# A graph network on one core: GpSimd's wait in the edge loop moved to the middle of a step and put on VectorE's turn of the step in front

## The chip, the cores and the metric

One NeuronCore of a Trainium2 chip. The metric is the time of one execution on the device, in microseconds (us); lower is better. The profiled execution and the timed runs are different executions of the same program.

## What is computed

Four layers of message passing on a graph with 6250 nodes and 206,250 directed edges, 64 channels, all in float32. The edges are sorted by target. In one layer:

```
msg   = relu(h[src] + e) + 1e-7            # one row of 64 per edge; e = edge_attr @ w + b
m     = msg * t
ex    = exp(m - segment_max(m, dst)[dst])
alpha = ex / segment_sum(ex, dst)[dst]
agg   = segment_sum(msg * alpha, dst)
out   = relu(layernorm((h + agg) @ w1 + b1)) @ w2 + b2
```

A small encoder stands before the layers, and layers 1 to 3 take `relu(layernorm(h))` and add their result to `h`. The gather `h[src]` fetches a 256-byte row of a table in HBM for every edge, once in each layer.

## The kernel before

**Streams and steps.** The edges are cut into four streams of equal length, each of which lies on 32 partitions (lanes). A *step* (`chunk` in the code) takes 256 edges of each stream. A layer has 202 steps, numbered k = 0 to 201; over all layers the number is n = 202 * layer + k. Two neighbouring steps make a pair, for which the large transfers are made. Layer 0 is written out apart from layers 1 to 3, which share one loop body: there `layer` is a register, and in layer 0 it is the Python number 0. The first four steps of a layer and the last ones are written out too, with k known, and those between are in a loop of four steps.

**A step, engine by engine.**
- GpSimd gathers the table's rows: eight indirect DMAs (L543), b = 0 to 7, each of 128 rows and 32 KB, into one of four places, that of n mod 4 (`gathered`, two buffers of two halves). Each adds 16 to the semaphore `rows_in[i]`, i = n mod 4. The last step of a layer has only four such blocks (`LAST_BLOCKS` = 4).
- VectorE waits for `rows_in` and *turns* the step (`turn_edges`, L1140, a stream transpose from `gathered` into PSUM), which adds 1 to `turn_done`. After that the place in `gathered` may be written again. It adds the edge terms (L1149), takes the running maxima (scans, L1161), the differences (L1175), the weighting (L1180), the running sums (scans, L1188 and L1193), and turns the sums into `rows_out` (L1203).
- ScalarE does the ReLUs and exponentials, and copies the indices of a later pair (`copy_idx`, `idx_ready`).
- SyncE has, for each pair, a store of `rows_out` (1024 KB), a load of `edges` (640 KB) and a store of `track` (513 KB). The first waits for `rows_ready`, which VectorE's L1203 gives, the other two for `scanned`, which its maxima (L1161) give.

**VectorE's order.** In the loop VectorE works on several steps at a time (`chunk` in its block): maxima of n-2, the turn of n, the turned sums of n-4, differences of n-2, weighting of n-3, edge terms of n, sums of n-3. From step 196 on (`CLOSE` = 197) the order is another: for k = 198 to 201 it is

```python
for k in range(CLOSE + 1, CHUNKS):
    peak(k - 1)      # maxima and differences
    leave(k - 2)     # turned sums, L1203
    turn(k)          # L1140
    add(k)
    sums(k - 1)      # weighting and sums
```

**GpSimd's order.** Its instructions are in order. `hold` is a wait for a semaphore followed by an increment of `pool_passed`, which nobody waits for in the loop. Ahead of the first step of a pair it holds for the indices; ahead of every step from k = 2 on it holds for `turn_done` to reach n - 1, which says that step n - 2 has been turned. The place that step n writes was last read by the turn of step n - 4.

At the end of a layer GpSimd waits for the stores of `track`, gathers a few rows for the streams' seams (L554, `head_parts`), and then one row for every node (L572).

Of the kernel before, what the change touches and what calls it, by code (L numbers as in the profile page):

```python
# [19 lines left out]
BLOCKS = N // LANES  # L20
# [62 lines left out]
def build_program(nc, x, src, dst, dst_blocks, few, ids, attr, enc_w, edge_w, w1, w2, rows, columns, final_row, consts, out):  # L83
# [17 lines left out]
    with ctx:  # L101
# [3 lines left out]
        def sem(name):  # L105
            return ctx.enter_context(nc.semaphore(name))
# [152 lines left out]
        turn_done = sem("turn_done")  # L259
# [64 lines left out]
        pool_passed = sem("pool_passed")  # L324
# [11 lines left out]
        def hold(eng, passed, s, count):  # L336

            if not (isinstance(count, int) and count <= 0):
                eng.wait_ge(s, count)
                eng.sem_inc(passed, 1)  # L340

        def chunk_quads(eng, layer, body, tail=2):

            for i in range(4):
                body(layer * CHUNKS + i, i, 0, i, False)
            with eng.Fori(1, (CHUNKS - tail) // 4) as j:
                for i in range(4):
                    body(layer * CHUNKS + 4 * j + i, 4 * j + i, j, i, False)
            for k in range(CHUNKS - tail, CHUNKS):
                body(layer * CHUNKS + k, k, k // 4, k % 4, k == CHUNKS - 1)  # L350
# [24 lines left out]
        def table_stores(layer):  # L375

            return 16 * (GROUPS + NODE_GROUPS * layer)

        def all_layers(eng, body):
            body(0)  # L380
            with eng.Fori(1, LAYERS) as layer:
                body(layer)
# [4 lines left out]
        def counts_until(t):  # L387

            g = t // GROUP
            done = sum(len(group_of(i)) for i in range(g % 2, g, 2)) + t - GROUP * g + 1
            return (counted_dve if g % 2 else counted_act), done
# [125 lines left out]
        @block.gpsimd  # L519
        def _(pool):  # L520
            for t in range(SEEK):
                hold(pool, pool_passed, block_found, t // GROUP + 1)
                if t >= GROUP:
                    hold(pool, pool_passed, *counts_until(t - GROUP))
                pool.indirect_dma_start(
                    found_rows[t % GROUP], None, dst_blocks,
                    bass.IndirectOffsetOnAxis(ap=block_i[:, t:t + 1], axis=0)).then_inc(block_in[t % GROUP], 16)

            def layer_body(layer):
                hold(pool, pool_passed, table_out, table_stores(layer))  # L530

                def chunk(n, k, j, i, last):
                    u, st = i // 2, i % 2
                    if st == 0:
                        hold(pool, pool_passed, idx_ready, PAIRS * layer + (2 if isinstance(k, int) and k == 0 else 2 * j + u + 1))

                    if not isinstance(k, int) or k >= 2:

                        hold(pool, pool_passed, turn_done, n - 1)
                    for b in range(LAST_BLOCKS if last else BLOCKS):  # L540
                        at = W * st + C * b
                        col = BLOCKS * st + b
                        pool.indirect_dma_start(  # L543
                            gathered[u][:, at:at + C], None, table,
                            bass.IndirectOffsetOnAxis(ap=idx_s[u][:, col:col + 1], axis=0)).then_inc(rows_in[i], 16)

                chunk_quads(pool, layer, chunk)

                for u in range(2):
                    hold(pool, pool_passed, track_stored[u], 16 * SLOT_PAIRS[u] * (layer + 1))  # L550
                if isinstance(layer, int):
                    pool.wait_ge(head_ready, 1)
                for i in range(4):
                    pool.indirect_dma_start(  # L554
                        head_parts[:, i:i + 1], None, tracks,
                        bass.IndirectOffsetOnAxis(ap=head_i[0:HEADS, i:i + 1], axis=0)).then_inc(heads_in, 16)
                for u in range(2):
                    hold(pool, pool_passed, rows_stored[u], 16 * SLOT_PAIRS[u] * (layer + 1))
                for i in range(2):
                    pool.indirect_dma_start(  # L560
                        head_rows[:, C2 * i:C2 * i + C2], None, state[0:EDGE_ROWS, :],
                        bass.IndirectOffsetOnAxis(ap=head_row_i[0:TARGETS, i:i + 1], axis=0)).then_inc(heads_in, 16)
                hold(pool, pool_passed, empty_out, 16)
                if isinstance(layer, int):
                    pool.wait_ge(end_ready, 1)
                hold(pool, pool_passed, merged_stored, 16 * (layer + 1))
                for i in range(NODE_GROUPS):

                    if i >= 2:
                        hold(pool, pool_passed, pre_ready, layer * NODE_GROUPS + i - 1)  # L570
                    for tile in range(FIRST[i], FIRST[i] + WIDTHS[i]):
                        pool.indirect_dma_start(  # L572
                            ends[:, tile, :], None, state,
                            bass.IndirectOffsetOnAxis(ap=end_i[:, tile:tile + 1], axis=0)).then_inc(ends_part[i], 16)

            all_layers(pool, layer_body)
# [903 lines left out]
```

## Time and profile before

| | |
|---|---|
| median of 3 runs | 8689.54 us (8688.6 to 8689.72) |
| the profiled execution | 8691.99 us |
| its span | 8690.2 us |
| VectorE busy | 6377.8 us (73%) |
| GpSimd busy | 6358.8 us (73%) |
| ScalarE busy | 3267.7 us (38%) |
| TensorE matmuls busy | 1037.5 us (12%) |

The span is that of the profile; the execution's own time is 1.8 us longer. In the profile's rows PE is TensorE, DVE is VectorE, ACT is ScalarE, POOL is GpSimd and SP is SyncE; the Lxxx is the line of the kernel. A gather's row on POOL is the time in which GpSimd makes the transfer's descriptors; the data land later.

### The profile page before, as it was taken

To read this page: it belongs to the slowest core of one execution; us is meant where nothing else is said; L and a number is where in the kernel's file an instruction comes from. 1 tells how busy PE (TensorE), PEld (TensorE's weight loads), DVE (VectorE), ACT (ScalarE), POOL (GpSimd) and SP (SyncE) were. 2 spreads that over 40 slices of the span, in tenths; PEclk is the share of its full clock that TensorE was granted. 3 is DMA by queue.
4 is the path that set the end of the run, shared out by engine and by line. 5 is a ranking of instruction groups with operands and counts; after the bars stand their busy time and mean duration, and the time that the engine had idled before them with its cause. 6 is when DMAs were issued, how large, how long until landed. Compare 5 with 4: busy or idle time off the path is not lost.

```text
span 8690.2 us, 45214 instructions
## 1 busy us (share of the span) xinstructions
PE 1037.5 (12%) x3019; PEld 763.4 (9%) x3019; DVE 6377.8 (73%) x10058; ACT 3267.7 (38%) x7146; POOL 6358.8 (73%) x6723
## 2 busy tenths in 40 slices
PE   4333333332200000000110000000020000000002
PEld 3222222221200000000110000000020000000002
DVE  6777777777677777777767777777776777777776
ACT  4444444443433333333333333333343333333334
POOL 6777777776677777777667777777756777777775
PEclk6655555555555555555555555555555555555555
DMA  6566555564244444444334444444433444444443
GB/s 202 206 206 206 203 201 203 202 203 163 89 136 136 138 139 139 139 139 136 120 97 139 138 135 136 138 139 139 139 109 105 139 139 138 135 136 137 139 139 106
DMA packets 444022, 1287.55 MB, mean 148 GB/s; under 512 B 164252, under 2 KB 178245, under 8 KB 366149
## 3 DMA queue, kind: packets, MB, share of 16 engines
q1 hardware_dynamic: 226516, 1049.15, 34.4%
q0 software_dynamic: 217456, 237.95, 10.8%
q14 instruction: 43, 0.34, 0.0%
q8 instruction: 7, 0.11, 0.0%
HBM read 574.47 MB, written 712.10 MB: 148 GB/s over the span
## 4 chain that ended last, share of the span: by engine, by line
POOL 24%; issue 16%; DVE 13%; DMA 13%; ACT 8%; PE 2%; POOLq 0%; ACTq 0%; DVEq 0%
POOL gathered L543 23%; DMA gathered<-node_table,idx_s 12%; DVE rows_out L1203 4%; ACT track L785 3%; DVE psum L1180 2%; DVE psum L1149 2%; ACT psum L792 2%; DVE psum L1175 2%; ACT psum L808 1%; DVE psum L1140 1%; PE psum L673 1%; PE psum L665 0%; ACT idx_s L776 0%; ACT square_junk L855 0%; POOL arena L572 0%
## 5 line engine op out<-in xcount | busy, mean ns | idle before, releaser
L543 POOL DMA_INDIRECT gathered<-node_table,idx_s x6448 | 6091.2, 945 | 2066.7 <-issue 1902.7
L800 ACT ACTIVATE decay<-psum 128x512 f32<-128x512 f32 (+1 forms) x808 | 481.7, 596 | 4893.2 <-DVE psum L1175 4893.2
L1140 DVE STREAM_TRANSPOSE psum<-gathered 128x512 f32<-128x512 f32 (+1 forms) x808 | 582.5, 721 | 2063.9 <-DMA gathered<-node_table,idx_s 2063.5
L1161 DVE TENSOR_TENSOR_SCAN track<-psum,track,edges 128x256 f32<-128x256 f32 (+1 forms) x1616 | 1107.3, 726 | 0.0
L1188 DVE TENSOR_TENSOR_SCAN run<-decay,run,psum 128x256 f32<-128x256 f32 (+1 forms) x1616 | 1100.4, 720 | 0.0
L1193 DVE TENSOR_TENSOR_SCAN run<-decay,run,psum 128x256 f32<-128x256 f32 (+1 forms) x1616 | 1094.5, 718 | 0.0
L1203 DVE STREAM_TRANSPOSE rows_out<-run 128x1024 f32<-128x1024 f32 (+1 forms) x808 | 970.3, 1201 | 0.1
L588 PE MATMUL psum<-attr_s,edgew_s 128*128 128x256 f32 x1616 | 748.4, 643 | 1259.8 <-ACT made_s L710 1246.2
L785 ACT ACTIVATE track<-psum,bias_col 128x256 f32<-128x256 f32 (+1 forms) x1616 | 678.7, 471 | 223.2 <-DVE psum L1149 174.8
L651 PE MATMUL psum<-cst,tails 128*3 128x128 f32 x48 | 10.9, 415 | 6160.6 <-DVE tails L1284 6091.0
L588 PEld LDWEIGHTS psum<-attr_s,edgew_s 128*128 128x128 f32 x1616 | 503.1, 326 | 1503.4 <-ACT made_s L710 1375.1
L1149 DVE TENSOR_TENSOR psum<-psum,edges 128x512 f32<-128x512 f32 (+1 forms) x808 | 558.4, 691 | 1.0
L1180 DVE TENSOR_TENSOR psum<-track,psum 128x512 f32<-128x512 f32 (+1 forms) x808 | 552.9, 684 | 3.3 <-ACT psum L808 3.2
L792 ACT ACTIVATE psum<-track,t_col 128x512 f32<-128x512 f32 (+1 forms) x808 | 551.5, 682 | 0.9
L651 PEld LDWEIGHTS psum<-cst,tails 128*3 128x3 f32 x48 | 5.6, 121 | 6165.8 <-issue 6162.4
L1175 DVE TENSOR_TENSOR psum<-track,psum 128x512 f32<-128x512 f32 (+1 forms) x808 | 538.3, 666 | 1.0
L807 ACT ACTIVATE decay<-decay 128x512 f32<-128x512 f32 (+1 forms) x808 | 506.2, 626 | 0.9
L808 ACT ACTIVATE psum<-psum 128x512 f32<-128x512 f32 (+1 forms) x808 | 480.1, 594 | 0.0
L801 ACT ACTIVATE psum<-psum 128x512 f32<-128x512 f32 (+1 forms) x808 | 477.5, 591 | 0.0
L572 POOL DMA_INDIRECT arena<-edge_state,end_i x196 | 185.2, 945 | 112.5 <-issue 65.8
L1337 DVE RECIPROCAL psum<-arena 128x448 f32<-128x448 f32 (+2 forms) x32 | 83.5, 2611 | 75.9 <-DMA arena<-edge_state,end_i 75.2
L710 ACT ACTIVATE made_s<-psum 128x512 f32<-128x512 f32 x202 | 119.1, 590 | 8.6 <-PE psum L588 8.6
(177 smaller groups left out, 1370.9 us busy)
## 6 DMA issues: line engine op xcount, KB each, us to landing
edge_state<-rows_out SPq DMA_DIRECT2D x404, 1024.0 KB, 5.1
edges<-edge_rows SPq DMA_DIRECT2D x406, 640.0 KB, 6.8
tracks<-track SPq DMA_DIRECT2D x404, 513.0 KB, 8.0
gathered<-node_table,idx_s POOLq DMA_INDIRECT x6448, 2.4
edge_rows<-made_s SPq DMA_DIRECT2D x101, 640.0 KB, 6.8
attr_s<-in_attr SPq DMA_DIRECT2D x101, 512.0 KB, 7.7
made_s<-resets SPq DMA_DIRECT2D x101, 128.0 KB
node_table<-tab SPq DMA_DIRECT2D x27, 224.0 KB, 2.5
```

Of the source, the lines that this page charges most:

```text
L543: pool.indirect_dma_start(gathered[u][:, at:at + C], None, table, bass.IndirectOffsetOnAxis(ap=idx_s[u][:, col:col + 1], axis=0)).then_inc ...
L588: last = pe.matmul(made_ps[:, N * q:N * q + N], edgew_s[:, col:col + P], attr_s[u][:, at:at + N], start=(half == 0), stop=(half == 1))
L785: last = act.activation(message[u][:, at:at + width], turned[s][:, N * q:N * q + width], ACT.Relu, bias=bias_col[:, q:q + 1])
L792: act.activation(halves(logit[s])[:, :, 0:width], halves(message[u])[:, :, N * st:N * st + width], ACT.Copy, scale=t_col[:, :]).then_inc(l ...
L1140: v.transpose(turned[s].rearrange("p (q b e) -> p b q e", q=2, e=LANES)[:, 0:blocks], gathered[u][:, W * st:W * st + C * blocks]).then_inc ...
L1149: v.tensor_tensor(sums, sums, halves(edges[u][:, W * st:W * st + W])[:, :, 0:width], ALU.add).then_inc(summed, 1)
L1161: last = v.tensor_tensor_scan(maxima[u][:, at:at + width], logit[s][:, N * q:N * q + width], reset_s[u][:, N * st:N * st + width], carried ...
L1175: v.tensor_tensor(logits, before, logits, ALU.subtract).then_inc(diff_done, 1)
L1180: v.tensor_tensor(halves(wmsg)[:, :, 0:width], halves(message[u])[:, :, N * st:N * st + width], halves(weight[s])[:, :, 0:width], ALU.mult ...
L1188: v.tensor_tensor_scan(run[s][:, N * q:N * q + width], decay[s][:, N * q:N * q + width], weight[s][:, N * q:N * q + width], run[1 - s][:, ...
L1193: last = v.tensor_tensor_scan(run[s][:, W + N * q:W + N * q + width], decay[s][:, N * q:N * q + width], wmsg[:, N * q:N * q + width], run[ ...
L1203: v.transpose(rows_out[u][:, 2 * W * st:2 * W * st + 2 * W].rearrange("p (b x c) -> p x b c", x=4, c=LANES)[:, :, 0:blocks], run[s][:, :]. ...
```

## The change

In layer 0 nothing changes. In layers 1 to 3 the hold for `turn_done` ahead of a step goes away. In its place one stands between the fourth and the fifth gather (b = 4) of every step but k = 0, and it is for `turn_done` to reach n, which says that step n - 1 has been turned.

```diff
-                    if not isinstance(k, int) or k >= 2:
+                    first = isinstance(layer, int)
+                    if first and (not isinstance(k, int) or k >= 2):
 
                         hold(pool, pool_passed, turn_done, n - 1)
                     for b in range(LAST_BLOCKS if last else BLOCKS):
+                        if not first and b == BLOCKS // 2 and not (isinstance(k, int) and k == 0):
+
+                            hold(pool, pool_passed, turn_done, n)
                         at = W * st + C * b
                         col = BLOCKS * st + b
                         pool.indirect_dma_start(
```

`first` is true in layer 0. `BLOCKS // 2` is 4. The last step's loop runs over b = 0 to 3 only.

## Rows read from the trace of the kernel before

**Rows 1.** The page, costliest groups: busy us, mean ns | idle before them.

```profile
L543 POOL DMA_INDIRECT gathered<-node_table,idx_s x6448 | 6091.2, 945 | 2066.7 <-issue 1902.7
```

**Rows 2.** Windows, layer 1's loop: busy us (instructions) of PE, PEld, DVE, ACT, POOL.

```profile
2270.00:4210.00 1940.00, 0.00 (x0) 0.00 (x0) 1447.70 (x2224) 699.52 (x1456) 1466.86 (x1554) 0.50 0.42 137
```

**Rows 3.** Waits of VectorE, same window: us in total, times, longest.

```profile
DVE psum L1140 <- DMA gathered<-node_table,idx_s: 495.5, 193, 7.3
```

**Rows 4.** Timeline, a pair of steps in layer 1's loop: start us, us.

```profile
4001.75 0.35 SPq L465 DMA_DIRECT2D edge_state<-rows_out  x1
...
4007.34 0.94 POOL L543 DMA_INDIRECT gathered<-node_table,idx_s  x1 [0.30 <-issue]
...
4011.34 0.73 DVE L1140 STREAM_TRANSPOSE psum<-gathered 128x512 f32<-128x512 f32 x1 [4.10 <-DMA gathered<-node_table,idx_s]
...
4013.59 0.94 POOL L543 DMA_INDIRECT gathered<-node_table,idx_s  x1 [0.30 <-issue]
...
4019.77 0.73 DVE L1140 STREAM_TRANSPOSE psum<-gathered 128x512 f32<-128x512 f32 x1 [0.97 <-DMA gathered<-node_table,idx_s]
```

**Rows 5.** Timeline, the end of layer 1's edge loop.

```profile
4227.06 0.69 DVE L1140 STREAM_TRANSPOSE psum<-gathered 128x512 f32<-128x512 f32 x1
...
4238.82 0.68 DVE L1140 STREAM_TRANSPOSE psum<-gathered 128x512 f32<-128x512 f32 x1
...
4240.31 0.95 POOL L543 DMA_INDIRECT gathered<-node_table,idx_s  x1 [2.07 <-DVE psum L1140]
...
4246.55 0.69 DVE L1140 STREAM_TRANSPOSE psum<-gathered 128x512 f32<-128x512 f32 x1
...
4252.44 0.34 SPq L424 DMA_DIRECT2D edges<-edge_rows  x1
...
4254.04 0.95 POOL L543 DMA_INDIRECT gathered<-node_table,idx_s  x1 [0.30 <-issue]
...
4254.21 0.68 DVE L1140 STREAM_TRANSPOSE psum<-gathered 128x512 f32<-128x512 f32 x1
...
4261.94 0.42 DVE L1140 STREAM_TRANSPOSE psum<-gathered 128x256 f32<-128x256 f32 x1
```

**Rows 6.** Windows, within the end of layer 1's edge loop.

```profile
4226.00:4260.00 34.00, 0.00 (x0) 0.00 (x0) 33.80 (x51) 15.28 (x31) 20.78 (x22) 0.50 0.58 189
```

**Rows 7.** Timeline, start of layer 1: turn of step 0, b4 of step 1.

```profile
2251.09 0.73 DVE L1140 STREAM_TRANSPOSE psum<-gathered 128x512 f32<-128x512 f32 x1 [8.76 <-DMA gathered<-node_table,idx_s]
...
2254.96 0.94 POOL L543 DMA_INDIRECT gathered<-node_table,idx_s  x1 [0.30 <-issue]
```

**Rows 8.** Timeline, a pair of steps in layer 3's loop.

```profile
7170.12 0.73 DVE L1140 STREAM_TRANSPOSE psum<-gathered 128x512 f32<-128x512 f32 x1 [5.20 <-DMA gathered<-node_table,idx_s]
...
7171.17 0.94 POOL L543 DMA_INDIRECT gathered<-node_table,idx_s  x1 [0.30 <-DVE psum L1140]
```

**Rows 9.** The chain: ahead of layer 1's first gather, and of its head_parts.

```profile
2238.91 1.08 issue
...
4267.27 4.17 DMA tracks<-track
4271.65 0.75 issue
```

**Rows 10.** L543 alone, whole execution: landings of its transfers.

```profile
DMA to landing us min/median/max: 2.3/2.4/8.1
```

**Rows 11.** L543 alone, last gather of layers 1, 2, 3: start, landing.

```profile
DMA to landing us min/median/max: 4.9/4.9/4.9
...
L543 POOL DMA_INDIRECT gathered<-node_table,idx_s x1: 946/946/946, 6401.6 to 6401.6; - x1
...
DMA to landing us min/median/max: 5.1/5.1/5.1
...
L543 POOL DMA_INDIRECT gathered<-node_table,idx_s x1: 943/943/943, 8550.5 to 8550.5; - x1
...
DMA to landing us min/median/max: 5.2/5.2/5.2
```

**Rows 12.** Timeline of VectorE, end of layers 2 and 3: turn of step 200.

```profile
6401.77 0.68 DVE L1140 STREAM_TRANSPOSE psum<-gathered 128x512 f32<-128x512 f32 x1
...
8550.60 0.69 DVE L1140 STREAM_TRANSPOSE psum<-gathered 128x512 f32<-128x512 f32 x1
```

## The prediction

> **What bounds the kernel now.** I read the page first [rows 1]: GpSimd's gathers (L543) are 6448 instructions of 945 ns, with 2066.7 us of short pauses between them, and nearly all of those pauses are not put down to a wait. The windows view of one layer's loop gives GpSimd's rate [rows 2]: 1940 us for 1554 gathers, 1.248 us each, so 9.99 us for a step of 8. In the same stretch VectorE waits 495.5 us, about 5 in each pair of steps, all of it ahead of its turn of a step (L1140) and for a gather [rows 3]. So GpSimd feeds VectorE.
>
> The timeline of a pair shows where they lie [rows 4]. I call a step by its number in its layer (0 to 201), b0 to b7 its gathers. The numbering is read backwards from the end of the layer: the last four gathers are step 201's, the pause before the row at 4240.31 stands at step 200's b0 [rows 5], and from there it goes by 1.249 us. So 4007.34 is b7 of step 176 and 4008.59 would be b0 of 177. The turn of 176 starts at 4011.34, 4.0 us after b7, because SyncE's three large transfers, the first issued at 4001.75, delay the landing; the turn of 177 starts at 4019.77, 2.43 us after b7 of 177 (4007.34 + 8 x 1.249 = 4017.34). Even steps are turned late and odd ones early, but GpSimd never pauses: its 0.30 us between gathers is there whether or not it had a wait to pass. Its queue is filled far ahead of it, so today's wait (turn of n-2 before b0 of n) is passed long before the gather is due: the turn of 176 ends at 4012.07, and step 178 begins four gathers after the row at 4013.59, at 4018.59, 6.5 us later.
>
> At the end of a layer VectorE leaves this rhythm. Steps 197 to 201 are done in another order, and the window 4226 to 4260 has 33.80 us of VectorE work in 34.00 us [rows 6]. There VectorE sets the end, not GpSimd.
>
> **The change, part by part.** No work is added. In layers 1 to 3 each step from 1 to 200 waits once, as steps 2 to 201 did before, now ahead of b4 and for the turn of n-1. Step 201 has four gathers, never comes to b4, and has no wait.
>
> *What a passed wait costs.* Where GpSimd did pause, the turn of 198 ran 4238.82 + 0.68 = 4239.50, and the gather held by it started at 4240.31 [rows 5]: 0.81 us from the end of the turn to the gather, after an empty queue. From there to the gather at 4254.04 it is 13.73 us for 11 gathers, 1.248 each, so running dry doesn't slow the ones behind it.
>
> *In the loop, odd n* (held by a late, even turn). Turn of 176 ends 4012.07, plus 0.81 is 4012.88; b4 of 177 now starts at 4013.59 [rows 4]. It is in time by 0.71 us. *Even n*: 4019.77 + 0.73 + 0.81 = 4021.31 against b4 of 178 at 4013.59 + 8 x 1.25 = 4023.59, 2.28 us in time. So the typical pair loses nothing, but on the odd side the margin is thin. I subtracted the same way for all 591 pairs of an L1140 and an L543 row in the three loops (steps 1 to 197 of each; the first pair of layer 1 stands in [rows 7]: 2251.09 + 0.73 + 0.81 = 2252.63 against 2254.96): odd margins have a mean of 0.64 us and go below zero some ten times, the worst being the turn at 7170.12 [rows 8]: 7170.85 + 0.81 = 7171.66 against 7171.17, 0.49 us late. The shortfalls sum to 0.1, 0.2 and 0.7 us: **1.0 us** for the three layers. A shortfall moves GpSimd, the next turn and the next large transfers alike, so the margin afterwards is the same: they add, and don't feed themselves. The other bound is a slower restart: ahead of a layer's first gather the chain has 1.08 us where the quick one has 0.75 [rows 9]. With all margins 0.33 us smaller the same sum is about 11 us. I take the quick one, since it is the in-loop case.
>
> *At the end of the layer* (layer 1; all from rows 5). The turns of 197, 198, 199, 200 start at 4227.06, 4238.82, 4246.55, 4254.21 and last 0.69. Step by step:
> - b4 of 198 would be due at 4223.5, and now waits for the turn of 197: 4227.75 + 0.81 = 4228.56. b7 at 4232.3. Landed long before 4238.82.
> - b0 of 199 follows at 4233.55, b3 at 4237.3. b4 waits for the turn of 198: 4240.31, the very time at which step 200 begins today. b7 at 4244.06; a quiet landing (2.4 us [rows 10]) is 4246.5, and VectorE wants it at 4246.55. No or little loss. Should it land up to 2.9 us later, that delay lies inside the next one, and adds at most 0.6 us.
> - b0 of 200 at 4245.31, b3 at 4249.05. The turn of 199 is over at 4247.24, so b4 to b7 go on without pause: b7 at 4254.05. That is four gathers later than today (4240.31 + 7 x 1.249 = 4249.05), and it is the time of today's last gather of all, which stands at 4254.04. It starts behind SyncE's transfers of 4252.44 and just after, triggered by scans of VectorE that lie ahead of the turn of 200 and don't move. So I take that gather's landing: 4.9 us [rows 11], 4259.0. VectorE wants it at 4254.21. **Late by 4.8 us.**
> - Step 201's four gathers end at 4259.05, land by 4261.5 to 4264, and are wanted at 4261.94 + 4.8. No further loss.
>
> Everything behind the turn of 200 on VectorE is in order and has no idle time to give back, and GpSimd's next instruction (the head_parts gather) comes behind a 4.17 us transfer of tracks that VectorE's last scan triggers [rows 9]. So the 4.8 us reach the end of the layer. Layers 2 and 3 have the same shape [rows 11, 12]: today's last gather at 6401.6 lands after 5.1 us = 6406.7 against a turn at 6401.77 (4.9); 8550.5 + 5.2 = 8555.7 against 8550.60 (5.1). Together 14.8 us, and 0.03 us of reaction each: **14.9 us**.
>
> The landing is the one disputed price. Its bounds are 2.4 us (the median of all) and 5.2 us. With 2.4 the gather lands at 4256.45, 2.2 us late, and three layers cost 6.6. I take 5, because those very rows start at the same point behind the same transfers.
>
> The Trainium skill (DMA: Bandwidth & Descriptors, section on the anatomy of one DMA on the gpsimd path) gives such a transfer about 2.0 us plus its bytes over 436 GB/s. For 32 KB that is 2.08 us by the page, an estimate; the quiet 2.4 us of this trace is near it, the 4.9 to 5.2 us behind large transfers are not. By the page each layer would lose 1.9 us and the whole change come to about 6.8 us.
>
> **Sum.** 1.0 + 14.9 = 15.9 us. The profiled execution took 8691.99 (span 8690.2 and 1.8 around it), and becomes 8707.9. It stands 2.5 above the median of the runs, so the median goes from 8689.54 to **8705.4**, 0.18% more. Nothing can be gained in the loop: GpSimd makes no pause there that a later wait could remove.
>
> **Rivals.**
> - *The loop stalls too.* If a wait in the middle restarts as slowly as a layer's first gather, or large transfers jitter more once GpSimd has no lead, the odd margins of 0.64 us are used up. At 0.33 us less it is 11 + 14.9 = 26 us, 8715.5; at 0.8 us less my pairs give 72 us, 8777. For it: the longest wait for a gather is 7.3 us in [rows 3], so late turns vary by microseconds. Against: every restart within the loop's end took 0.81.
> - *The last gather lands quietly.* Condition: the transfers of 4252.4 don't hold it. 1.0 + 6.6 = 7.6 us, 8697. Against: [rows 11].
> - *Nothing happens.* The 4.8 us would have to be hidden in the layer's end, or step 200's gathers be sent earlier than I count. 8689.5 to 8691. Against: the 33.80 busy of 34.00 [rows 6].
> - *Faster.* With fewer gathers queued the 1.249 us interval might shrink. It pays from 3.3 ns each (15.9 us over 4848 gathers); at 10 ns it is 8657. Against: the gathers after the restart, with nothing queued behind them, are 1.248 us apart.
>
> **How the numbers follow.** My forecast 0.66, its own range 8702.5 to 8710 (landings of 4.5 to 5.5 us, loop stalls of 0 to 5). Stalls in the loop 0.17, quiet landing 0.07, nothing 0.06, faster 0.04. A time can be told from no change here from about 0.2% on, 17.4 us, or 8706.9. My forecast lies just inside it: of its 0.66 I put 0.46 below and 0.20 above. Same: 0.46 + 0.07 + 0.06 = 0.59. Slower: 0.20 + 0.17 = 0.37. Faster 0.04. The range reaches down to the quiet landing (8696) and up to the slow restart (8716); outside are nothing, faster, and the worse half of the loop stalls, 0.18.
>
> **What would show it.** In the changed profile: GpSimd's interval stays 1.25 us in the three loops, with pauses over 0.35 us in some ten steps and none beyond 0.6; at a layer's end three pauses (b4 of 198, 5 us; b4 of 199, 2 to 3 us; then none until the layer's last gather, near 5 us later than today counted from the layer's start); VectorE idle for 4.8 to 5.1 us before the turn of 200, where it now has no idle time; the loop's waits of VectorE near 495 us. Layer 0 stays as it is. I am wrong if most pairs show a pause before b4, if that turn doesn't wait, or if the wait is given back before the layer ends.

## The result, and the profile of the changed kernel

Median 8706.93 us over 13 runs, against 8688.6 us over 13 runs of the kernel before: 18.3 us more, a ratio of 1.0022 with a 95% interval of [1.0014, 1.0029]. The forecast was 15.9 us more. The change makes the kernel slower, by 0.21%, just above the 0.2% from which the prediction takes a time as told from no change.

The profiled execution took 8706.93 us (span 8705.1), 14.9 us more than the one before (8691.99), which had been 3.4 us above the median of the 13 runs. On the page, the gathers have the same duration as in [rows 1] and their pauses add up to 22 us more; VectorE waits for them as before.

```profile
L547 POOL DMA_INDIRECT gathered<-node_table,idx_s x6448 | 6085.9, 944 | 2089.0 <-issue 2006.5
L1144 DVE STREAM_TRANSPOSE psum<-gathered 128x512 f32<-128x512 f32 (+1 forms) x808 | 582.6, 721 | 2081.5 <-DMA gathered<-node_table,idx_s 2081.5
```

(The change added four lines, so L543 is now L547 and L1140 is L1144.) The window over layer 1's loop, the same as in [rows 2], has the same 1554 gathers in 1940 us. The next line is the wait of VectorE there, 492.8 us against 495.5 in [rows 3]. In the loop, then, next to nothing has changed.

```profile
2270.00:4210.00 1940.00, 0.00 (x0) 0.00 (x0) 1447.16 (x2225) 699.49 (x1456) 1465.42 (x1554) 0.50 0.45 137
```

```profile
DVE psum L1144 <- DMA gathered<-node_table,idx_s: 492.8, 194, 8.0
```

Now the end of layer 1's edge loop, which answers to [rows 5]. All times here are about 2 us earlier than in the trace before, because the layer began that much earlier. Start us, us, engine, line, and in brackets the idle time before.

```profile
4225.05 0.68 DVE L1144 STREAM_TRANSPOSE psum<-gathered 128x512 f32<-128x512 f32 x1
4226.54 0.94 POOL L547 DMA_INDIRECT gathered<-node_table,idx_s  x1 [5.92 <-DVE psum L1144]
...
4236.82 0.68 DVE L1144 STREAM_TRANSPOSE psum<-gathered 128x512 f32<-128x512 f32 x1
4238.31 0.94 POOL L547 DMA_INDIRECT gathered<-node_table,idx_s  x1 [2.08 <-DVE psum L1144]
...
4244.57 0.73 DVE L1144 STREAM_TRANSPOSE psum<-gathered 128x512 f32<-128x512 f32 x1
...
4250.49 0.34 SPq L424 DMA_DIRECT2D edges<-edge_rows  x1
...
4252.03 0.94 POOL L547 DMA_INDIRECT gathered<-node_table,idx_s  x1 [0.30 <-issue]
...
4257.02 0.94 POOL L547 DMA_INDIRECT gathered<-node_table,idx_s  x1 [0.30 <-issue]
4257.26 0.73 DVE L1144 STREAM_TRANSPOSE psum<-gathered 128x512 f32<-128x512 f32 x1 [4.92 <-DMA gathered<-node_table,idx_s]
```

The four VectorE rows are the turns of steps 197, 198, 199 and 200 (4225.05, 4236.82, 4244.57, 4257.26; the first pause of GpSimd is ahead of b4 of 198, the second ahead of b4 of 199). In [rows 5] the turn of 200 came 7.66 us after that of 199 with no idle time; here it comes 12.69 us after, 4.92 of them idle. The last gather of step 200 (4252.03; the one at 4257.02 is the last of 201) goes 1.5 us after SyncE's load of edges. The chain of the three layers has what that gather took from its start to its landing:

```profile
4252.03 5.20 DMA gathered<-node_table,idx_s
...
6405.94 4.83 DMA gathered<-node_table,idx_s
...
8561.64 5.13 DMA gathered<-node_table,idx_s
```

In the window 4224 to 4258 VectorE now has 28.90 us of work, where [rows 6] had 33.80 in 34.00.

```profile
4224.00:4258.00 34.00, 0.00 (x0) 0.00 (x0) 28.90 (x42) 13.75 (x28) 22.64 (x24) 0.50 0.61 188
```

In the loops GpSimd makes some short pauses that weren't there. The worst is in layer 3, ahead of b4 of an odd step, and answers to [rows 8]: the turn that it waits for ends at 7339.86, and 0.80 us later the gather starts, in place of 0.30 us after its predecessor.

```profile
7339.00 0.94 POOL L547 DMA_INDIRECT gathered<-node_table,idx_s  x1 [0.30 <-issue]
7339.13 0.73 DVE L1144 STREAM_TRANSPOSE psum<-gathered 128x512 f32<-128x512 f32 x1 [5.09 <-DMA gathered<-node_table,idx_s]
7340.66 0.94 POOL L547 DMA_INDIRECT gathered<-node_table,idx_s  x1 [0.71 <-issue]
```

Counted over all rows of the gathers and turns, layer by layer (loop: steps 1 to 196, pauses above 0.35 us and what they have above 0.30; end: from the end of the turn of 196 to that of 200):

| layer | before: pauses, end | changed: pauses, end |
|---|---|---|
| 0 | 1 (0.4 us), 42.94 | 1 (0.4 us), 42.94 |
| 1 | 0, 42.88 | 7 (1.1 us), 47.98 |
| 2 | 0, 42.87 | 5 (1.0 us), 47.61 |
| 3 | 0, 42.88 | 10 (2.4 us), 47.91 |

The ends of layers 1 to 3 take 5.10, 4.74 and 5.03 us more, 14.9 together, and the loops' pauses come to 4.6 us. Their sum, 19.5, stands beside the 18.3 of the medians. The two profiled executions are only 14.9 us apart because the loops of layers 1 to 3 were themselves a little long in the trace before: from the turn of step 4 to that of 196 they took 1919.96 to 1920.49 us there, and 1918.5 to 1919.8 us in the other kernels whose loops have no pause. The changed kernel's took 1920.35, 1920.65 and 1921.87.

### The profile page after: what moved, and what is told of

Read it like the earlier page. It is cut to its first block, busy times and chain, and to the rows that moved or that the text cites. A ratio compares the mean times of both kernels' runs of the same rounds, so it can differ in the third digit from the quotient of the medians.

```text
span 8705.1 us, 45361 instructions
## 1 busy us (share of the span) xinstructions
PE 1039.3 (12%) x3019; PEld 770.2 (9%) x3019; DVE 6378.0 (73%) x10058; ACT 3267.4 (38%) x7146; POOL 6353.2 (73%) x6723
## 4 chain that ended last, share of the span: by engine, by line
POOL 44%; issue 21%; DMA 5%; DVE 3%; PE 2%; ACT 1%; POOLq 0%; DVEq 0%
POOL gathered L547 43%; DMA gathered<-node_table,idx_s 4%; DVE psum L1144 1%; PE psum L677 1%; PE psum L669 0%; ACT square_junk L859 0%; POOL arena L576 0%; PE psum L686 0%; DVE run L1197 0%; POOLq L346 0%; DVE run L1192 0%; DVE track L1165 0%; POOL head_parts L558 0%; DVE pre L1351 0%; DVE psum L1348 0%
## 5 line engine op out<-in xcount | busy, mean ns | idle before, releaser
L547 POOL DMA_INDIRECT gathered<-node_table,idx_s x6448 | 6085.9, 944 | 2089.0 <-issue 2006.5
L1144 DVE STREAM_TRANSPOSE psum<-gathered 128x512 f32<-128x512 f32 (+1 forms) x808 | 582.6, 721 | 2081.5 <-DMA gathered<-node_table,idx_s 2081.5
```

The costliest lines, as they stand in the source:

```text
L547: pool.indirect_dma_start(gathered[u][:, at:at + C], None, table, bass.IndirectOffsetOnAxis(ap=idx_s[u][:, col:col + 1], axis=0)).then_inc ...
L1144: v.transpose(turned[s].rearrange("p (q b e) -> p b q e", q=2, e=LANES)[:, 0:blocks], gathered[u][:, W * st:W * st + C * blocks]).then_inc ...
```

## Experiments

Each has runs of the kernel before beside it, from the same chip; "end" is the stretch of the table above, of layers 1, 2 and 3. Single runs of one kernel spread over some 8 us, so the ends and pauses in the traces say more than the medians here.

**Only the loop changed.** Steps 198 to 201 keep the wait of before; for that, the last six steps are written out.

```diff
-                    first = isinstance(layer, int)
-                    if first and (not isinstance(k, int) or k >= 2):
+                    moved = not isinstance(layer, int) and not (isinstance(k, int) and k >= 198)
+                    if not moved and (not isinstance(k, int) or k >= 2):
...
-                        if not first and b == BLOCKS // 2 and ...
+                        if moved and b == BLOCKS // 2 and ...
...
-                chunk_quads(pool, layer, chunk)
+                chunk_quads(pool, layer, chunk, tail=6)
```

> In layers 1 to 3 steps 1 to 197 wait as in the changed kernel (ahead of b4, for the turn of n-1), steps 198 to 201 as in the kernel before. My theory (the loop costs only the few short pauses of a margin that runs out, the end of a layer the rest): the three loops take 1 to 5 us longer together, the stretch from the turn of step 196 to that of 200 stays at 42.9 us, and the time is 1 to 5 us above the kernel before. Rival (every wait in the middle of a step costs a little): most of the 18 us stays.

8689.31 against 8687.22, ratio 1.0002 [0.9993, 1.0011]. Ends 42.89, 42.89, 42.88. Pauses 7, 4 and 3, together 2.9 us. The end is cured, and the short pauses of the loop stay. By the medians alone, 2.1 us can't be told from nothing.

**Only the end changed.** The same with `isinstance(k, int) and k >= 198` as the condition for `moved`.

> The reverse: only steps 198 to 200 have the changed wait (201 none), all others that of the kernel before. My theory: the loops are as before, from the turn of 196 to that of 200 it is 47.6 to 48.0 us in place of 42.9, three times, so 14 to 16 us above the kernel before. Rival (loop): within 3 us of the kernel before.

8701.85 against 8687.22: 14.6 us, ratio 1.0015 [1.0006, 1.0024]. Ends 47.71, 47.74, 47.90, 14.7 us above 42.88 together. No pause in the loops. With the run before this splits the change into its two parts: 14.6 and 2.1 by the medians.

**Only the place changed, not the turn that is waited for.**

```diff
-                        if not first and b == BLOCKS // 2 and not (isinstance(k, int) and k == 0):
+                        if not first and b == BLOCKS // 2 and not (isinstance(k, int) and k < 2):
 
-                            hold(pool, pool_passed, turn_done, n)
+                            hold(pool, pool_passed, turn_done, n - 1)
```

> The wait stands ahead of b4 in layers 1 to 3, but is still for the turn of step n-2. My theory: it is passed more than 10 us ahead of its gather in the loop, and at a layer's end the first pause comes later than before, so no difference: within 2 us of the kernel before, no pause of GpSimd in the loops. Rival (the place costs, since a wait breaks a run of gathers): 10 us or more above.

8687.52 against 8687.22, ratio 1.0 [0.9991, 1.0009]; ends 42.88, 42.88, 42.87; no pause in the loops. A wait within a step costs nothing by itself that these runs could show.

**The wait one gather earlier, ahead of b3.**

```diff
-                        if not first and b == BLOCKS // 2 and ...
+                        if not first and b == 3 and ...
```

> As the changed kernel, with the wait one gather earlier (ahead of b3). My theory: the mean margin of 0.64 us on the odd side becomes a lack of 0.6, so every odd step pauses; the pair is then even turn after odd turn 11.7 us, plus 0.81 restart, four intervals of 1.249, 2.43 landing and 0.73 turn, 20.65 in place of 19.98 us: 0.66 us x 98 pairs x 3 = 195 us, and about 18 us at the ends: 8900 us, give or take 25. Rival (the margin is no such quantity, a wait costs by its count): the time stays near 8707.

8915.89 against 8687.22: 228.7 us, ratio 1.0257 [1.0241, 1.0272]. One gather (1.25 us) of margin less makes the loss twelve times as large. The timeline in layer 1's loop:

```profile
3302.47 0.73 DVE L1144 STREAM_TRANSPOSE psum<-gathered 128x512 f32<-128x512 f32 x1 [4.12 <-DMA gathered<-node_table,idx_s]
3304.01 0.94 POOL L547 DMA_INDIRECT gathered<-node_table,idx_s  x1 [0.92 <-DVE psum L1144]
...
3311.38 0.73 DVE L1144 STREAM_TRANSPOSE psum<-gathered 128x512 f32<-128x512 f32 x1 [1.45 <-DMA gathered<-node_table,idx_s]
...
3323.46 0.73 DVE L1144 STREAM_TRANSPOSE psum<-gathered 128x512 f32<-128x512 f32 x1 [4.56 <-DMA gathered<-node_table,idx_s]
3324.99 0.94 POOL L547 DMA_INDIRECT gathered<-node_table,idx_s  x1 [1.32 <-DVE psum L1144]
...
3332.49 0.73 DVE L1144 STREAM_TRANSPOSE psum<-gathered 128x512 f32<-128x512 f32 x1 [1.57 <-DMA gathered<-node_table,idx_s]
```

Nearly every late (even) turn is followed by a pause of GpSimd, 3302.47 + 0.73 + 0.81 = 3304.01, and the odd turns wait longer than in [rows 4]. Over the loops an odd turn follows 9.00 us after the even one (sum of the forecast: 8.97) and an even one 11.63 to 11.72 after the odd one. There are 94 or 95 pauses in each layer. The loops take 63, 71 and 71 us more (forecast 65 each): where the even turns are at 11.72 a pair loses 0.72 us and not 0.66. The ends are 49.10, 48.90 and 49.16, 18.5 us more together (forecast 18). That is 223 us in the profile, 229 by the medians, against 213 and a bound of 238.

**Only step 199 changed**, in each of layers 1 to 3, with the last six steps written out as above.

```diff
+                    moved = not isinstance(layer, int) and isinstance(k, int) and k == 199
```

> In each of layers 1 to 3 one step alone, 199, has the changed wait, all others that of the kernel before. My theory: its b4 then goes at the time at which b0 of step 200 went, which puts step 200 four gathers later and its last gather behind SyncE's transfers, by itself: the whole 14 to 16 us, 4.7 to 5.1 in each layer. Rival (each of the changed waits at the end adds its share): about a third of it, 5 us.

8699.76 against 8686.73: 13.0 us, ratio 1.0015 [1.0006, 1.0024]. Ends 47.88, 47.71 and 48.09, as with all steps changed; no pause in the loops. Three waits of some 600 do the damage. In the timeline of layer 1's end GpSimd now stops once, ahead of b4 of 199, until the same time as with the changed kernel (end of the turn of 198 plus 0.81):

```profile
4236.42 0.68 DVE L1144 STREAM_TRANSPOSE psum<-gathered 128x512 f32<-128x512 f32 x1
...
4237.91 0.94 POOL L547 DMA_INDIRECT gathered<-node_table,idx_s  x1 [7.02 <-DVE psum L1144]
```

**The wait two gathers later, ahead of b6** (`b == 6`).

> As the changed kernel, with the wait ahead of b6. My theory: the odd margins of the loop grow by 2.5 us to about 3.1, so no pause there; at a layer's end step 200's last gather goes 2.5 us after its time before, at 4251.55 by the times of the kernel before, in front of SyncE's transfers of 4252.4, and lands about when the turn of 200 is due: 0 to 0.5 us late. In all 0 to 2 us above the kernel before. Rival (a late wait costs by its count, wherever it stands): 15 to 20 us above.

8687.66 against 8686.73, ratio 1.0001 [0.9992, 1.001]. No pause in the loops; ends 42.93, 43.66 and 43.05. Only in layer 2 is the turn of 200 noticeably late, and then by little:

```profile
6403.33 0.73 DVE L1144 STREAM_TRANSPOSE psum<-gathered 128x512 f32<-128x512 f32 x1 [0.65 <-DMA gathered<-node_table,idx_s]
```

**The changed kernel, with one of SyncE's transfers out of the way.** The load of edges that goes 1.5 us ahead of step 200's last gather is issued at the end of the layer.

```diff
                     if not final:
-                        load_edges(after, u)
+                        held_back = isinstance(m, int) and m == PAIRS - 2 and not isinstance(layer, int)
+                    if not final and not held_back:
+                        load_edges(after, u)
...
                         store_rows(n, m, u)
                         load_edges(after, u)
+                        if not isinstance(layer, int):
+                            load_edges(1, 1)
```

> The changed kernel, and in layers 1 to 3 the load of edges (640 KB) that SyncE issues just ahead of the last gather's landing (after the maxima of step 199) is issued at the very end of the layer instead. My theory (the landing of 4.9 to 5.2 us is paid to those transfers): the last gather of step 200 lands in 2.4 to 4.2 us, and from the turn of 196 to that of 200 it is 45 to 47 us in place of 47.6 to 48.0; 3 to 8 us less than the changed kernel. Rival (that landing is long for another reason): no difference to the changed kernel.

8698.32 against 8686.73: 11.6 us, ratio 1.0013 [1.0004, 1.0022], and 6.7 us less than the changed kernel's 18.3 (each against its own runs of the kernel before). Ends 45.18, 45.21 and 45.55; pauses in the loops 0, 2 and 8, together 2.1 us. The turn of 200 in layer 1 waits 2.18 us in place of 4.92, and the chain has a landing of 2.40 us in place of 5.20:

```profile
4255.74 0.73 DVE L1147 STREAM_TRANSPOSE psum<-gathered 128x512 f32<-128x512 f32 x1 [2.18 <-DMA gathered<-node_table,idx_s]
```

```profile
4253.32 2.40 DMA gathered<-node_table,idx_s
```

So of the 5 us of each end, 2.3 to 2.7 are GpSimd's lateness, and the rest is that transfer, behind which the last gather now comes.

**The wait ahead of b0** (`b == 0`), so that nothing of a step is gathered before the turn of the one in front.

> As the changed kernel, with the wait ahead of b0, so that GpSimd has no step in hand. My theory, by the same terms: an odd turn comes 0.81 + 7 x 1.249 + 2.43 + 0.73 = 12.7 us after the even one, an even turn as long after the odd one or a little more, since its last gather goes 9.55 us after and the large transfers are then nearly through: 25.4 us for a pair in place of 19.98, 5.4 x 98 x 3 = 1590 us, some 25 at the ends: 10300 us, give or take 100. Rival (VectorE hides part of it): under 1000 us more.

10386.9 against 8686.73: 1700 us, ratio 1.1956 [1.1934, 1.1978]. Every step pauses some 3 us:

```profile
3311.30 0.73 DVE L1144 STREAM_TRANSPOSE psum<-gathered 128x512 f32<-128x512 f32 x1 [5.19 <-DMA gathered<-node_table,idx_s]
3312.83 0.94 POOL L547 DMA_INDIRECT gathered<-node_table,idx_s  x1 [2.97 <-DVE psum L1144]
...
3321.58 0.94 POOL L547 DMA_INDIRECT gathered<-node_table,idx_s  x1 [0.30 <-issue]
3323.96 0.73 DVE L1144 STREAM_TRANSPOSE psum<-gathered 128x512 f32<-128x512 f32 x1 [5.13 <-DMA gathered<-node_table,idx_s]
```

An odd turn comes 12.67 us after the even one (forecast 12.7), an even one 12.94 after the odd one. The loops take 550 us more each (forecast 530), the ends 16 each (forecast 25 for the three together).

**The least wait, for the turn of n-4.** In layers 1 to 3, ahead of b0, on the kernel before.

```diff
-                    if not isinstance(k, int) or k >= 2:
+                    if not isinstance(k, int) or k >= (2 if isinstance(layer, int) else 4):
 
-                        hold(pool, pool_passed, turn_done, n - 1)
+                        hold(pool, pool_passed, turn_done, n - (1 if isinstance(layer, int) else 3))
```

> In layers 1 to 3 the wait ahead of a step from 4 on is for the turn of n-4, the least that keeps the places in gathered apart. My theory (GpSimd's 1.249 us interval bounds the loop, and VectorE the end): more lead buys nothing, within 2 us of the kernel before, and no pause of GpSimd in the loops. Rival (the lead still limits somewhere, so that a way to gain exists): 5 us or more below the kernel before.

These runs were unlike all the others: the kernel before took 10019 us beside them. This kernel took 10173.35, ratio 1.0153 [1.014, 1.0166]. The same kernel was run once more, on another chip:

> The kernel of e9_least_wait once more, since in its runs the kernel before took 10019 us, 15% more than in all others, and so didn't show what lead buys at the usual speed. My theory: where the kernel before takes some 8687 us, GpSimd makes no pause in the loops and the time is within 2 us of it. Rival (more lead puts gathers in the way of other transfers, as it may have there): slower by 10 us or more.

8688.35 against 8688.3, ratio 0.9999 [0.999, 1.0008]; no pause in the loops of layers 1 to 3, ends 42.88 in each. Where the kernel before takes its usual 8687 to 8689 us, more lead buys nothing and costs nothing.

**Two more beside a kernel before of 10019 us.** The wait ahead of b5 (`b == 5`):

> As the changed kernel, with the wait ahead of b5. My theory: odd margins of 1.9 us in the loop, so no pause there; the last gather of step 200 goes 1.25 us sooner than in the changed kernel and lands in up to 5.3 us, 3 to 4 us after VectorE wants it: from the turn of 196 to that of 200 it is 45.5 to 47 us, 8 to 12 us above the kernel before. Rival (a landing that is either in front of the transfers or behind them): no loss, or the same 5 us per layer as with b4.

10011.9 against 10019.0, ratio 0.9986 [0.9977, 0.9996].

And the changed wait everywhere but in step 199 (`not (isinstance(k, int) and k == 199)` as the condition for `moved`):

> The changed wait in all steps of layers 1 to 3 but 199, which has the wait of the kernel before. My theory: step 198 still pauses until 4228.56 (in the times of the kernel before), but step 199 then runs on, and step 200's last gather goes at about 4252.3 in place of 4254.05: 0.6 to 3.5 us late in a layer, so from the turn of 196 to that of 200 43.5 to 46.4 us, 2 to 10 us at the ends and 1 to 3 in the loops. Rival (199 is the only step that costs): the ends as in the kernel before, 42.9.

9991.81 against 10019.0, ratio 0.9975 [0.9966, 0.9985]. Neither answers its question, since the ends of those executions can't be laid beside the others: even in layer 0, whose code is the same in every kernel, the end takes 46.80 and 43.46 us in these two and 51.11 in the least wait's, where it is 42.94 to 42.96 in all other traces. Whether the stop of step 198 alone costs anything stays open, and so does b5. The timeline of the last kernel shows another rhythm. SyncE's three transfers of a pair are issued over 5.7 us, where those of [rows 4] take 1.1 (4001.75 to 4002.89), and GpSimd pauses in the loop.

```profile
3504.80 0.36 SPq L465 DMA_DIRECT2D edge_state<-rows_out  x1
3507.44 0.02 SPq L424 DMA_DIRECT2D edges<-edge_rows  x1
3510.45 0.71 SPq L485 DMA_DIRECT2D tracks<-track  x1
...
3516.19 0.95 POOL L547 DMA_INDIRECT gathered<-node_table,idx_s  x1 [2.46 <-remote]
```

What those three kernels do say: the order turned round there. The least wait was the slowest, and the waits within the step were a little faster than the kernel before. Layer 0 was slow in all three alike (from the turn of step 4 to that of 196 it took 2307 to 2317 us, against 1914), and the least wait lost its time in the loops of layers 1 to 3 (2232 to 2237 us each, the other two 2176 to 2190). Why those executions took 15% more, and whether fewer gathers in flight were what helped there, is open. They ran on the chip numbered 3, and so did the first four experiments, at the usual speed.

## Why the prediction was right, and where it was off

- *GpSimd's interval sets the loop, and its lead hides the wait.* Shown: least wait, place only and b6 make no pauses in the loops and no difference in time.
- *A passed wait restarts in 0.81 us.* Shown at every pause quoted: 4225.73 to 4226.54, 3303.20 to 4.01, 7339.86 to 40.66. Of the 890 pauses ahead of b4, b3 or b0 in the loops of the changed kernel and of its variants with b3 and b0, 881 end 0.80 to 0.82 us after the turn; the other nine, all at step 8, 9 or 12 of a layer, take 1.01 to 1.08. The rival of a slow restart (1.08 us) falls.
- *Margins of 0.71 and 2.3 us; the odd side is thin.* Shown by the dose: ahead of b6 and b4 (2.5 us apart) it goes from no pause to 22 in three layers, ahead of b3 to 283, ahead of b0 all steps pause.
- *The loop loses 1.0 us.* **This is the term that was mis-sized**: 4.6 us in the profile of the changed kernel, 2.9 with only the loop changed, 2.1 with the load of edges out of the way. Why is told below. My ten pauses became 22, the worst 0.71 us against a forecast limit of 0.6. That limit didn't fit its own rows: the gather that is 0.49 us late would make a pause of 0.79.
- *The end of a layer loses 4.8, 4.9 and 5.1 us.* Measured 5.10, 4.74 and 5.03 and, with only the end changed, 4.83, 4.87 and 5.02. Its steps hold too: the stop of step 198 isn't needed, since step 199 alone gives the whole loss, and nothing is given back later (from the turn of 200 to that of 201 it is 7.46 us before and after, and from there to the next layer's first gather, or in layer 3 to the last instruction, 383.2 us in three layers before and 383.0 changed).
- *The last gather's landing is 4.9 to 5.2 us behind SyncE's transfers, not a quiet one.* 5.20, 4.83 and 5.13; with the load of edges taken away, 2.40. The rule that the forecast weighed (the Trainium skill, DMA: Bandwidth & Descriptors, section on the anatomy of one DMA on the gpsimd path) is thus near for a quiet transfer (2.08 us, an estimate by its formula; 2.40 here), and off by more than a factor of two for one behind large transfers.
- The sum was 15.9 against 18.3. The missing 2.4 us are no more than what the loop's term was short of (3.6 by the changed kernel's profile, 1.9 by that with only the loop changed), and they carry the result from just below the line of 0.2% to just above it. With any of the five other readings of the loop's term the sum would have been 16.8 to 18.9 us. Nothing in the one trace before could tell which, so how near 15.9 comes to 18.3 is in part chance.
- Two slips without effect on the sum: layers 1 to 3 have 4836 gathers and not 4848, and of the "three pauses" at a layer's end the text lists two, which are the two that came (5.92 and 2.08 us).

**Where the loop's term went wrong.** The shortfalls were summed over one execution, and that one was the most favourable. The same sum over the rows of the other kernels whose loops have no pauses gives 1.9 us (only step 199), 2.7 (b6), 3.3 (place only), 3.8 (least wait, at the usual speed) and 4.0 (only the end). It is also steep: with every margin 0.1 us smaller the rows of the trace before give 2.9 us, with 0.2 smaller 5.6. The average turn doesn't tell it. The even turn came 11.81 us after the odd one in the changed kernel's loops and 11.69 in the trace before, but also 11.69 with only the loop changed, which had 2.9 us of pauses.

What goes with it is the share of the time that the packets of the gathers' queue took. The page has these lines, before and changed:

```profile
q0 software_dynamic: 217456, 237.95, 10.8%
...
q0 software_dynamic: 217456, 237.95, 12.8%
```

In the other traces of the usual speed (b3 and b0 left out, whose loops are longer) that share is 11.3% where the sum or the pauses come to 1.9 to 2.7 us, and 12.1 or 12.2% where they come to 2.9 to 4.0. It goes with the set of runs that a trace was taken in and not with the wait: 11.3% with only step 199, with b6 and with the load of edges held back; 12.1% with only the loop, only the end and only the place; 12.2% with the least wait. So the forecast read a thin margin at one end of a spread between executions, and the changed kernel's profile stood at the other. That the packets' time is the cause of the thinner margins is not shown.

## What to carry to other kernels

- A wait that nobody feels can stand next to a cliff. Work out its margin, as the time at which the held instruction would go anyway less the time at which it is let go plus the restart, for each place of the loop, and its spread: here 2.5 us more margin cost nothing and 1.25 us less cost 210 us more.
- Look at the ends of a loop by themselves. Where another engine leaves its rhythm, the margin of the steady state says nothing: 3 of some 600 waits made some three quarters of this loss (13.0 of 18.3 us by the medians, 15.1 of 19.5 in the traces).
- When a delayed transfer lands, ask what is issued in between: half of the loss at each end was not the delay but a large transfer that had slipped in front.

## What the runs showed of the hardware that was not expected

- On one occasion every kernel ran 15% slower (the kernel before 10019 us against 8687), on a chip of a number that was at the usual speed before (3), with GpSimd's gathers at the same 0.95 us and the same 0.30 between them, but with SyncE's issues drawn out from 1.1 to 5.7 us for three. The order of the kernels by time was another there. A verdict on a few tenths of a per cent holds for the condition in which it was measured.
- The gathers' packets of 2 KB (16 for each gather) took 124 ns on average in the trace before, 130 in each of the traces of only step 199, b6 and the load of edges held back, 140 or 141 in those of the loop, the end and the place alone, of b3 and of the least wait, and 150 in the changed kernel's, although the medians of the kernel before stay within 8687 to 8690 us. So it differs between sets of runs and not between the kernels of one set, and not by the chip alone: chip 3, on which the loop, the end, the place and b3 had 140, showed 153 or 154 where everything took 15% longer. What sets it is open.
